# An attention kernel gets a tail of its own for its last two images: reciprocals spread by 32-row matmuls, four output banks, a split residual, two store queues

## What is computed

```python
xn = group_norm(x, gn1_w, gn1_b)
q, k, v = jnp.split(conv1x1(xn, w_qkv), 3, axis=1)      # 4 heads x 32 channels, n = 4096 tokens
q = jax.nn.elu(q) + 1.0
k = jax.nn.elu(k) + 1.0
k_sum = k.sum(axis=2)
kv = jnp.einsum('bhnd,bhne->bhde', k, v)
qk_sum = jnp.einsum('bhnd,bhd->bhn', q, k_sum)
out = jnp.einsum('bhnd,bhde->bhne', q, kv) / (qk_sum[..., None] + EPS_ATTN)
out = conv1x1(out, w_out)                                # 128 -> 64 channels
out = group_norm(out, gn2_w, gn2_b)
return out + residual                                    # residual = x, the result of the scans
```

## Time and profile before

| | |
|---|---|
| median of 3 runs | 727.37 us (727.2 to 728.03) |
| the profiled execution | 724.89 us |
| its span (first to last instruction) | 722.9 us |
| share of the span: PE, DVE, ACT, POOL | 88%, 79%, 64%, 19% |
| granted TensorE clock over the span | 0.958 |
| last use of PE | until 710.0 us |

### The profile page before, as it was taken

The page is one execution under the profiler, slowest core; times in us unless marked ns, Lnnn a source line. Parts: engine busy times, 40 slices in busy tenths (PEclk is TensorE's granted clock), DMA queues, the critical chain, the costliest instruction groups (busy, mean ns, idle before and its releaser), DMA issues.

```text
span 722.9 us, 27175 instructions
## 1 busy us (share of the span) xinstructions
PE 639.1 (88%) x10416; PEld 538.2 (74%) x10416; DVE 568.6 (79%) x1937; ACT 462.7 (64%) x1060; POOL 136.4 (19%) x110
## 2 busy tenths in 40 slices
PE   4899999999999899999999999299889889889641
PEld 4899999888898899999999998256555455456210
DVE  4899898888888798989999999678568687677352
ACT  3556667999999566666666666177647667666321
POOL 0024000000000000000000000101454954954702
PEclk9999999999999999999999999699999999999955
DMA  9999840000000000000000000003252573583586
GB/s 175 204 201 201 160 83 1 1 0 0 0 0 0 2 1 0 0 0 0 2 0 0 0 0 0 1 2 83 49 121 70 119 172 73 119 170 77 124 175 116
DMA packets 64874, 45.23 MB, mean 63 GB/s; under 512 B 42112, under 2 KB 56512, under 8 KB 64832
## 3 DMA queue, kind: packets, MB, share of 16 engines
q1 hardware_dynamic: 63616, 44.38, 30.9%
q10 hardware_dynamic: 1216, 0.30, 0.2%
HBM read 35.23 MB, written 9.44 MB: 62 GB/s over the span
## 4 chain that ended last, share of the span: by engine, by line
DVE 30%; PE 26%; issue 16%; POOL 12%; DMA 6%; ACT 6%; DVEq 2%; SPq 1%; ACTq 1%; POOLq 0%
PE bank L425 20%; DVE scan_rows L609 9%; POOL rows_h L373 9%; DVE parts L595 7%; DVE parts L609 7%; DMA rows_h<-bounce 3%; DVE tok L668 3%; ACT cols_w L854 3%; DMA bounce<-recip 2%; POOL fin L399 2%; ACT parts L838 2%; PE bank L549 1%; DVEq L609 1%; SPq L310 1%; DMA yn<-L_conv_k_td 1%
## 5 line engine op out<-in xcount | busy, mean ns | idle before, releaser
L425 PE MATMUL bank<-parts 128*128 128x124 f16 (+2 forms) x7560 | 433.8, 219 | 16.1 <-DVE parts L218 8.8
L425 PEld LDWEIGHTS bank<-parts 128*128 128x128 f16 x7560 | 417.9, 98 | 31.9 <-issue 12.5
L838 ACT ACTIVATE parts<-parts 128x128 f16<-128x128 f16 x508 | 157.1, 309 | 126.0 <-DVE parts L609 104.1
L595 DVE TENSOR_TENSOR parts<-scan_rows,parts 128x128 f16<-128x128 f32 x508 | 148.9, 293 | 14.3
L609 DVE SCALAR_TENSOR_TENSOR parts<-bank,cols_w 128x128 f16<-128x128 f32 x378 | 109.7, 290 | 20.3 <-PE bank L425 7.1
L609 DVE SCALAR_TENSOR_TENSOR scan_rows<-bank,cols_w 128x128 f32<-128x128 f32 x378 | 106.1, 281 | 0.1
L373 POOL TENSOR_TENSOR rows_h<-rows_h 128x512 f32<-128x512 f32 x56 | 79.9, 1457 | 106.0 <-DMA rows_h<-bounce 106.0
L854 ACT ACTIVATE cols_w<-scan_rows 64x256 f32 (+1 forms) x128 | 82.8, 647 | 2.3
L720 DVE SCALAR_TENSOR_TENSOR kp<-ex,bank 128x512 f32<-128x512 f32 x64 | 40.9, 680 | 45.6 <-ACT ex L926 45.6
L365 POOL TENSOR_TENSOR scale<-dev,half 128x8 f32<-128x8 f32 x1 | 1.7, 1675 | 389.0 <-DVE dev L701 389.0
L549 PE MATMUL bank<-rows_h,mix 128*64 128x512 f32 x128 | 38.1, 677 | 22.5 <-POOL rows_h L373 14.3
(11 more groups left out here) (104 smaller groups left out, 540.8 us busy)
## 6 DMA issues: line engine op xcount, KB each, us to landing
rows_h<-bounce SPq DMA_DIRECT2D x64, 256.0 KB, 4.9
cols_w<-x SPq DMA_DIRECT2D x12, 896.0 KB, 13.6
out<-fin SPq DMA_DIRECT2D x14, 512.0 KB, 7.9
cols_w<-x SPq DMA_DIRECT2D x6, 640.0 KB, 10.8
cols_w<-x SPq DMA_DIRECT2D x6, 256.0 KB, 6.6
bounce<-recip SPq DMA_DIRECT2D x16, 64.0 KB, 3.4
out<-rows_h SPq DMA_DIRECT2D x4, 256.0 KB, 4.4
scan_rows<-x SPq DMA_DIRECT2D x2, 128.0 KB, 4.1
```

The lines of the kernel that those rows point to most:

```text
L425: last = nc.tensor.matmul(conv_rows[g][u % SLOTS][:, :, to], w[:, k, d, :], rows_16[:, u % SLOTS, g * GB:(g + 1) * GB, of], start=part_n = ...
L595: nc.vector.tensor_tensor(low[:, slot, gb, :], state[:, slot, gb, :], high[:, slot, gb, :], ALU.subtract).then_inc(low_ready[g], 1)
L838: act.activation(high_down[:, slot, gb, :], high[:, slot, gb, :], ACT.Copy, scale=1.0 / LOW_SCALE).then_inc(down_ready[g], 1)
```

## The change

Iterations 8 and 9 are gone. Each engine has instead a `tail()` written out by hand for images 6 and 7.

- **Reciprocals of image 7** don't go through DRAM. A new constant `back_to_heads` (128 x 4 x 128, 256 KB, loaded by SP behind the broadcasts of image 1 into the dead state of the scans) is the weight of matmuls that take 32 rows each and write all 128 partitions: `reciprocals_back(m)`, 16 of them over 128 columns, with unit u in a bank of its own. DVE multiplies the units straight from those banks.
- **Denominators** of m = 1 go to `acc_ps` rather than `small_ps`, and `mix` has a second copy, `mix_last`.
- **Normalising**: image 6 by POOL as before; image 7 by DVE.
- **Outputs of image 7** go to four banks (`last_ps`). DVE takes the statistics from the banks, and ACT copies each chunk behind them.
- **ACT at the end of iteration 7**: the gather for image 7 comes ahead of the affine step of image 5.
- **Residual**: image 6 is POOL's in four quarters into `fin_tail[:, 0]`, with scale and shift of image 7 ahead of the last quarter. Image 7's first half is DVE's x * scale + residual followed by ACT's + shift; its second half is ACT's affine followed by DVE's sum.
- **Stores**: image 5 no longer waits for image 7's broadcasts, image 6 is stored in halves, and image 7's odd rows are issued by ACT.

The functions of the tail, engine by engine:

```diff
+        fin_tail = recip_b.rearrange("p u n -> p (u n)").rearrange("p (c j w) -> p c j w", c=2, j=J)
+        back_to_heads = scan_rows[:, 0:SUBS * P].rearrange("p (s n) -> p s n", s=SUBS)
+        back_ps = (key_ps[0], key_ps[1], query_ps[0], query_ps[1], acc_ps, key_ps[0], key_ps[1], query_ps[0])
+        last_den_ps = (small_ps, acc_ps)
+        last_ps = (out_ps, tok_ps, query_ps[1], acc_ps)
...
+            sp.dma_start(back_to_heads, consts[:, 3 * P + SUBS * DH:].rearrange("p (s n) -> p s n", s=SUBS))\
+              .then_inc(back_loaded, 16)
...
-            for m in range(2):
-                broadcast(B - 1, m)
-            for c in (B - 3, B - 2):
-                sp.wait_ge(fin_ready, c + 2)
-                store(c, slice(0, J))
+            sp.wait_ge(fin_ready, B - 1)
+            store(B - 3, slice(0, J))
             for h, rows in enumerate(HALVES):
-                sp.wait_ge(fin_ready, B + 1 + h)
-                store(B - 1, rows, fin_last)
-            sp.wait_ge(stored, 1 + 32 * (B + 1))
+                sp.wait_ge(fin_ready, B + h)
+                store(B - 2, rows, fin_tail[:, 0])
+            for h, rows in enumerate(HALVES):
+                sp.wait_ge(last_ready, h + 1)
+                store(B - 1, rows, fin_tail[:, 1], (0,))
+            sp.wait_ge(stored, 1 + 32 * (B + 2))
...
+            def residual(q):
+                pool.wait_ge(affine_done, B - 1 + q // 2)
+                rows = slice(q * J // 4, (q + 1) * J // 4)
+                last = nc.gpsimd.tensor_tensor(
+                    fin_tail[:, 0, rows, :].rearrange("p j w -> p w j"),
+                    proj[:, 0, :].rearrange("p (w j) -> p w j", j=J)[:, :, rows], cols[:, :, B - 2, rows], ALU.add)
+                if q % 2:
+                    last.then_inc(fin_ready, 1)
+            pool.wait_ge(tail_read, 6)
+            scale_and_shift(B, 0)
+            for q in range(3):
+                residual(q)
+            pool.wait_ge(tail_read, 8)
+            scale_and_shift(B + 1, 1)
+            residual(3)
...
+            def last_denominators(m):
+                for s in range(SUBS):
+                    for u in range(4):
+                        last = nc.tensor.matmul(last_den_ps[m][DH * u:DH * (u + 1), 0:SUB],
+                                                den_w[:, s * DH:(s + 1) * DH],
+                                                qp[:, 1, 4 * m + u, s * SUB:(s + 1) * SUB],
+                                                start=s == 0, stop=s == SUBS - 1)
+                last.then_inc(tail_done, 1)
+            def reciprocals_back(m):
+                pe.wait_ge(recip_ready, 2 * (B - 1) + m + 1)
+                for s in range(SUBS):
+                    for u in range(4):
+                        here = slice(DH * u, DH * (u + 1))
+                        last = nc.tensor.matmul(back_ps[4 * m + u][:, s * SUB:(s + 1) * SUB], back_to_heads[here, s, :],
+                                                recip[here, m, :], start=True, stop=True)
+                last.then_inc(back_done, 1)
+            def one_before_last(i):
+                pe.wait_ge(normed, UNITS * (B - 2) + 2 * i + 2)
+                for d in range(2):
+                    last = nc.tensor.matmul((out_ps, tok_ps)[i - 2][d * C:(d + 1) * C, :], mix[:, :], qp[:, 0, 2 * i + d, :],
+                                            start=True, stop=True)
+                last.then_inc(proj_done, 1)
+            def last_output(i):
+                pe.wait_ge(normed_last, 2 * i + 2)
+                for d in range(2):
+                    last = nc.tensor.matmul(last_ps[i][d * C:(d + 1) * C, :], mix_last[:, :], qp[:, 1, 2 * i + d, :],
+                                            start=True, stop=True)
+                last.then_inc(last_out, 1)
+            pe.wait_ge(small_read, small_step(B - 1, 5))
+            pe.wait_ge(proj_read, NCHUNK * (B - 2) + 2)
+            pe.wait_ge(acc_read, B)
+            sums().then_inc(tail_done, 1)
+            pe.wait_ge(tail_read, 1)
+            pe.wait_ge(qp_ready, UNITS * B)
+            for m in range(2):
+                last_denominators(m)
+            pe.wait_ge(tail_read, 2)
+            nc.tensor.matmul(small_ps[:, 0:C], kv[:, :], w_o[:, :], start=True, stop=True).then_inc(tail_done, 1)
+            one_before_last(2)
+            pe.wait_ge(back_loaded, 16)
+            pe.wait_ge(kp_ready, KBANKS * B)
+            reciprocals_back(0)
+            pe.wait_ge(tok_ready, 4 * B)
+            one_before_last(3)
+            pe.wait_ge(normed_last, 3)
+            pe.wait_ge(tail_read, 3)
+            reciprocals_back(1)
+            pe.wait_ge(tail_read, 4)
+            pe.wait_ge(proj_read, NCHUNK * (B - 2) + 3)
+            last_output(0)
+            pe.wait_ge(stat_ready, 2 * B - 1)
+            group_sums(agg2[:, 0:1]).then_inc(tail_done, 1)
+            pe.wait_ge(proj_read, NCHUNK * (B - 1))
+            last_output(1)
+            last_output(2)
+            pe.wait_ge(stat_ready, 2 * B)
+            pe.wait_ge(tail_read, 5)
+            group_sums(dev2[:, 2:3]).then_inc(tail_done, 1)
+            last_output(3)
+            pe.wait_ge(stat_ready, 2 * B + 1)
+            pe.wait_ge(tail_read, 6)
+            group_sums(agg2[:, 0:1]).then_inc(tail_done, 1)
+            pe.wait_ge(stat_ready, 2 * B + 2)
+            pe.wait_ge(tail_read, 7)
+            group_sums(dev2[:, 2:3]).then_inc(tail_done, 1)
...
+            def last_reciprocal(m):
+                dve.wait_ge(tail_done, 2 + m)
+                sum_ = (den, acc_g)[m]
+                nc.vector.tensor_scalar(sum_[:, :], last_den_ps[m][:, 0:SUB], EPS_ATTN, None, ALU.add)\
+                    .then_inc(tail_read, 1)
+                dve.wait_ge(tail_read, 2 + m)
+                dve.wait_ge(bounced, 16 * (2 * (B - 2) + m + 1))
+                nc.vector.reciprocal(recip[:, m, :], sum_[:, :]).then_inc(recip_ready, 1)
+            def last_normalised(u):
+                dve.wait_ge(back_done, u // 4 + 1)
+                nc.vector.tensor_tensor(qp[:, 1, u, :], qp[:, 1, u, :], back_ps[u][:, :], ALU.mult).then_inc(normed_last, 1)
+            def tail():
+                dve.wait_ge(tail_done, 1)
+                nc.vector.tensor_tensor(den_w[:, :], small_ps[:, 0:P], head_of, ALU.mult)
+                nc.vector.tensor_tensor(kv[:, :], small_ps[:, P:2 * P], same_head, ALU.mult).then_inc(tail_read, 1)
+                stats_before_last(0)
+                stats_before_last(1)
+                for m in range(2):
+                    last_reciprocal(m)
+                dve.wait_ge(tail_done, 4)
+                nc.vector.tensor_copy(mix_last[:, :], small_ps[:, 0:C]).then_inc(tail_read, 1)
+                stats_before_last(2)
+                for u in range(4):
+                    last_normalised(u)
+                stats_before_last(3).then_inc(norm2, 1)
+                aggregate_output(norm2, B - 1)
+                for u in (4, 5):
+                    last_normalised(u)
+                dve.wait_ge(affine_ready, B - 1)
+                deviation(5)
+                for u in (6, 7):
+                    last_normalised(u)
+                variance(6)
+                for i in range(NCHUNK):
+                    dve.wait_ge(last_out, i + 1)
+                    nc.vector.bn_stats(stats2[:, i, :], last_ps[i][:, :]).then_inc(last_stated, 1)
+                aggregate_output(last_stated, NCHUNK)
+                dve.wait_ge(affine_ready, B)
+                deviation(7)
+                variance(8)
+                first, second = HALVES
+                mine = lambda rows: proj[:, 1, :].rearrange("p (w j) -> p w j", j=J)[:, :, rows]
+                dve.wait_ge(last_read, NCHUNK)
+                dve.wait_ge(scale_ready, 2 * (B + 1))
+                nc.vector.scalar_tensor_tensor(out=fin_tail[:, 1, first, :].rearrange("p j w -> p w j"), in0=mine(first),
+                                               scalar=scale2[:, 1:2], in1=cols[:, :, B - 1, first], op0=ALU.mult,
+                                               op1=ALU.add).then_inc(last_sum, 1)
+                dve.wait_ge(last_affine, 1)
+                dve.wait_ge(last_ready, 1)
+                nc.vector.tensor_tensor(fin_tail[:, 1, second, :].rearrange("p j w -> p w j"), mine(second),
+                                        cols[:, :, B - 1, second], ALU.add).then_inc(last_ready, 1)
...
+            def tail():
+                gathered(B)
+                affine(B - 1, 1, slice(0, J))
+                for i in (2, 3):
+                    act.wait_ge(proj_done, NCHUNK * (B - 2) + i + 1)
+                    act.activation(proj[:, 0, chunk_of(i)], (out_ps, tok_ps)[i - 2][:, :], ACT.Copy).then_inc(proj_read, 1)
+                act.wait_ge(fin_ready, B - 1)
+                for i in range(NCHUNK):
+                    act.wait_ge(last_stated, i + 1)
+                    act.activation(proj[:, 1, chunk_of(i)], last_ps[i][:, :], ACT.Copy).then_inc(last_read, 1)
+                for rows in HALVES:
```

(43 more changed lines are left out.)

114 lines of the change are left out of this document (62 added, 52 removed).

## The result

| | before | changed |
|---|---|---|
| median | 727.7 us (727.2 to 728.05, 4 runs) | 715.25 us (714.28 to 715.69, 4 runs) |
| profiled execution, its span | 724.89 us, 722.9 us | 714.88 us, 712.9 us |
| tail | 48.6 us | 37.5 us |

The ratio is 0.983 with a 95% interval of 0.9803 to 0.9857: the changed kernel is 12.5 us faster in the medians and 10.0 us in the two profiles. All that the change touches lies behind it but one load, and it takes out the up to 2.4 us by which the profiled executions differ ahead of it.

A forecast was written before the change was run, and what follows sets the result against it. Image 7's reciprocals' DRAM round trip was taken to set the end of computing, stacked stores the end of the kernel. Span 722.9 to 712.5 us saves 10.4 us; median 727.37 - 10.4 = 717.0 us, range 713.8 to 721.5 us.

The forecast's parts named there:

- rival A: POOL's one-column shift for image 7 is not held by DVE; everything behind it 1.8 us earlier, 715.2 us; chance 0.15.
- Start 3.0 us earlier: Start of the tail: ACT's gather of image 7 comes first, so PE's sums and DVE's masks run 3.0 us earlier.
- No `bounce` transfer behind 670 us: Sign in the changed kernel's profile: no transfer of reciprocals through DRAM after 670 us.
- 1.1 us for a set of 32-row matmuls: PE's 16 matmuls of `reciprocals_back` run with row groups side by side, 1.1 us a set; upper bound 4.8 us.
- Rival C: The 32-row matmuls go one after another at 4.8 us a set, 7 us in all: 724 us; chance 0.08.
- DVE and PE interleaved to 689.1 us: DVE's products 0.64 us apart alternate with PE's sets and outputs of 1.08 us; units 6 and 7 done at 689.1 us.
- The clock holds until about 693 us: PE's clock stays at 1.00 up to about 693 us, its longest idle stretch from 677 to 690.6 us being 1.2 us.
- rival B: PE's clock falls despite shorter gaps, outputs take 1.99 instead of 1.08 us: 719.5 to 721.3 us; chance 0.15.
- POOL as what image 7's scale waits for: Image 7's scale queues behind POOL's three quarters of image 6's residual, 694.1 to 697.8 us; scale at 698.9 us.
- The shift held by DVE: POOL's shift for image 7 waits for DVE's 1.9 us two-SBUF-input sum, until 700.9 us, done at 701.2 us.
- The last sum at 705.6 us: DVE's sum of image 7's second half, behind ACT's affine and shift, ends at 705.6 us.
- Start, completion and 1.57 MB at 200 GB/s: 9.9 us: Three half stores from 702.6 us end the kernel: 2.0 us start and completion plus 7.9 us transfer, to 712.5 us.

The follow-up runs named there:

- u_turn: Changed kernel with the two loops of the 32-row matmuls exchanged, so one row group's matmuls follow each other: 721.23 us, ratio 0.9913, tail 45.4 us.
- t_psum: Changed kernel with DVE's product and sum for image 7's first half reading x from PSUM in four instructions: 712.64 us, ratio 0.9805, tail 35.9 us.
- v_combo2: Changed kernel, first half from PSUM, one store queue, own semaphore for second half, image 7's scale and shift before image 6's third quarter: 712.53 us, ratio 0.9801.
- t_oneq: Changed kernel with all four stores of image 7 issued by SP, none by ACT: 713.45 us, ratio 0.9816, tail 36.8 us.
- v_before: The kernel before, unedited, profiled a second time: 726.86 us, ratio 0.9996, tail 51.0 us.
- t_dram: Changed kernel with image 7's reciprocals through DRAM again and no 32-row matmuls, rest of the new tail kept: 725.5 us, ratio 0.9993, tail 49.2 us.
- v_combo4: Changed kernel, first half from PSUM, one store queue, own semaphore for second half, image 7's scale and shift behind all four quarters: 712.88 us, ratio 0.9817.
- t_affine1st: Changed kernel with ACT's affine of image 5 ahead of the gather of image 7 again: 718.15 us, ratio 0.988, tail 40.7 us.

## Why the prediction was right, point by point

Forecast 717.0 us, range 713.8 to 721.5 us; measured 715.25 us. The forecast's order of events was that of the profile. The measured median lies just below the 715.6 to 718.5 us that were to show the forecast, and on the 715.2 us of rival A, whose mechanism the trace refutes: the time alone could not have told them apart. Times below are the changed kernel's less the 1.1 us by which its anchor is later.

- **Start 3.0 us earlier.** DVE's masks at 676.4 us, forecast 676.5.
- **No `bounce` transfer behind 670 us.** Wrongly put as a sign: POOL waits for image 6's last one until 676.2 us in the changed kernel's own time, as it did until 674.9 us before. Image 7 has none.
- **1.1 us for a set of 32-row matmuls.** 1.17 us. Rival C fails in the changed kernel; u_turn shows what it would look like: its sets are 2.82 and 4.67 us.
- **DVE and PE interleaved to 689.1 us.** Units 6 and 7 were through at 687.8 us. 0.7 us of the 1.3 us were won before the first product (681.6 us, forecast 682.3). The rest: the products from PSUM are 0.61 us apart, not 0.64, and PE's outputs don't pay the full 1.08 us when they follow each other (two chunks in 1.94 us).
- **The clock holds until about 693 us.** It was 1.00 to 692 us and 0.50 from 694 us; rival B fails. What the forecast didn't have is the other side of that step: in one of two profiles the clock of the kernel before did not hold.
- **POOL as what image 7's scale waits for.** The first starts at 692.6 us, forecast 694.1. Three quarters take 3.68 us, forecast 3.7 us; the last starts at once behind the shift.
- **The shift held by DVE.** 1.97 us in place of 0.34, and 2.2 us from the scale's end to the shift's, forecast 2.3 us. Rival A fails, and t_psum shows the cause. v_combo2 has the same with POOL first. By the Trainium skill (SBUF — State Buffer, "Who interferes with whom") two SBUF inputs on DVE exclude a GpSimd instruction that reads SBUF; the traces agree, down to an instruction of one column.
- **The last sum at 705.6 us.** 703.8 us: the steps ahead of it had gained 1.8 us on the sum.
- **Start, completion and 1.57 MB at 200 GB/s: 9.9 us.** 11.1 us. This is the term that was mis-sized the other way. The stores moved at 182 GB/s, which makes 8.6 us instead of 7.9 (an estimate from the rate), and leaves 2.5 us for start and completion instead of 2.0. The rate of before's last 1.5 us, 226 GB/s, did not come with two queues. By the Trainium skill's rule (DMA: Bandwidth & Descriptors, "Issuing engines are not separate DMA queues") a second issuing engine saves only issuing time; t_oneq agrees, it lost nothing with one.
- **Sum 10.4 us.** The tails differ by 11.1 us. That the forecast came within 0.7 us of this is in part luck: POOL's last quarter ended 1.9 us sooner than forecast, and the stores behind it took 1.2 us longer.
- **The median from one profile.** The profiled spans differ by 10.0 us, the medians by 12.5 us. The forecast took the median of before and subtracted what one profile showed, in which the clock had happened to hold; v_before has a tail that is 2.3 us longer. Whether this is why the medians moved more than the profiles is open: the timed executions have no traces, and the profiled execution of v_before took 725.93 us, which is still below its median of 726.86 us.

## What to carry to other kernels

A DRAM round trip that is hidden in a steady loop is bare in the last iteration; there, a matmul with a 0/1 weight can do the spreading, and it paid twice here, since PE, which no longer waited for the transfers, kept its clock (4.1 us for the outputs instead of 7.9 in t_dram). Put the four row groups of 32-row matmuls next to each other in the queue, one bank each. The new order around it is worth nothing without it: t_dram had that order with the trip, and gained nothing. Before shortening the computing of a tail further, count the bytes from the first late store on: here seven profiles of six kernels ended 10.4 to 11.1 us behind the step that let this store go. Starting that store sooner helped (t_psum); with the later ones delayed as well (v_combo4) the DMA engines fell idle and it took 12.4 us.

## What was unexpected of the hardware

- An instruction of POOL on one column took 1.97 us beside a DVE instruction with two SBUF inputs, and 0.33 us beside DVE instructions that took one of them from PSUM. The other way round, a DVE sum with two SBUF inputs took 2.66 us beside an instruction of POOL that had started first (v_combo2), and 1.93 us without.
- The clock of one and the same kernel at one and the same place was 1.00 in one execution and 0.50 in another, behind idle stretches of PE of 3.31 and 3.79 us (the kernel before). Behind 1.23 us it was 1.00 in both profiles of the changed kernel, behind 3.21 us (t_affine1st) 0.50.
- Sixteen 32-row fp32 matmuls took 1.17 us with neighbours in different row groups and PSUM banks, and 2.82 us with neighbours in the same group and bank, both at the full clock.
- In u_turn the clock fell from 1.00 to 0.50 within the second set, while PE was recorded as busy for 0.50 of each 0.50 us from 685.0 to 686.0 us. It had been idle for 0.97 us ahead of the set; in the changed kernel, behind 1.09 us at the same place, the clock held.
